# Attention and a gated recurrence on one core: own gate banks for each token half, the attention of tiles 6 and 7 ended by halves

## The reference

```python
# attention of each tile, linear form
Q, K, V = x @ Wq.T + bq, x @ Wk.T + bk, x @ Wv.T + bv
Q, K = elu(Q) + 1, elu(K) + 1
KV = einsum('bnd,bne->bde', K, V)
Z = einsum('bnd,bd->bn', Q, K.sum(axis=1) + 1e-6)
x1 = layernorm(x + (einsum('bnd,bde->bne', Q, KV) / Z[..., None]) @ Wo.T + bo)
# recurrence over the tiles; c is 512 x 128
for t in range(8):
    f = sigmoid(x1[t] @ wf.T + c @ uf.T + bf)
    i = sigmoid(x1[t] @ wi.T + c @ ui.T + bi)
    g = tanh(x1[t] @ wc.T + c @ uc.T + bc)
    c = f * c + i * g
out = layernorm(x1 + tanh(x1 @ wo.T + c @ uo.T + bo))
```

## Time and profile before

| what | us |
|---|---|
| median of 3 runs (lowest, highest) | 103.58 (103.49, 103.77) |
| the profiled execution: time | 102.75 |
| its span, first to last instruction | 101.0 |
| busy: TensorE, VectorE, ScalarE, GpSimd | 91.6, 80.9, 68.5, 42.1 |

### The profile page before, as it was taken

How to read it: one execution, slowest core, us unless ns; L and a number is a source line. 1 busy time by engine, 2 the same in 40 slices (tenths; PEclk the granted TensorE clock), 3 DMA queues, 4 the chain that set the end, 5 groups by cost and what they waited for, 6 DMA issues and landing times.

```text
span 101.0 us, 1930 instructions
## 1 busy us (share of the span) xinstructions
PE 91.6 (91%) x607; PEld 78.8 (78%) x607; DVE 80.9 (80%) x234; ACT 68.5 (68%) x143; POOL 42.1 (42%) x65
## 2 busy tenths in 40 slices
PE   5989999999799999999999999999999999896700
PEld 4859879688488978978888999989899999785300
DVE  3256598979999996898689989996455999999970
ACT  1465767587497694785869445599365949889760
POOL 2004598148358058019306704260500055455870
PEclk9999999999999999999999999999999999999998
DMA  1869999100000000000000000000000000153366
GB/s 37 295 210 295 401 394 368 46 0 3 0 0 0 0 0 0 10 0 0 0 0 0 6 0 0 0 3 3 6 0 0 0 0 0 47 168 104 104 208 208
DMA packets 5413, 7.36 MB, mean 73 GB/s; under 512 B 507, under 2 KB 3228, under 8 KB 5404
## 3 DMA queue, kind: packets, MB, share of 16 engines
q1 hardware_dynamic: 4972, 6.92, 19.4%
q10 hardware_dynamic: 432, 0.33, 1.2%
HBM read 5.15 MB, written 2.10 MB: 72 GB/s over the span
## 4 chain that ended last, share of the span: by engine, by line
PE 57%; DVE 27%; issue 5%; ACT 4%; POOL 3%; DVEq 0%; POOLq 0%; ACTq 0%
PE ps_ctx L433 7%; PE ps_k L410 6%; PE ps_q L424 6%; PE ps_ctx L453 5%; DVE stats L1140 5%; PE ps_f L397 4%; DVE x L1129 3%; DVE x L960 3%; PE ps_x L467 2%; DVE s L1011 2%; DVE x L975 2%; DVE x L1156 2%; DVE new L1004 2%; PE ps_ctx L443 2%; PE ps_f L481 2%
## 5 line engine op out<-in xcount | busy, mean ns | idle before, releaser
L346 POOL TENSOR_TENSOR s_lo<-s,s_hi 128x512 fp32r<-128x512 f32 (+1 forms) x8 | 8.1, 1012 | 24.6 <-ACT s_hi L752 24.6
L333 POOL TENSOR_TENSOR rstd<-var_eps,minus_half 128x4 f32<-128x4 f32 (+1 forms) x9 | 9.1, 1010 | 12.6 <-DVE var_eps L1148 12.6
L317 POOL TENSOR_TENSOR rstd<-var_eps,minus_half 128x4 f32<-128x4 f32 x8 | 8.6, 1078 | 6.6 <-DVE var_eps L951 6.5
L308 POOL TENSOR_TENSOR k_pair<-k_rows 128x256 f32<-128x256 f32 x8 | 6.3, 782 | 9.1 <-DVE k_rows L986 9.1
L960 DVE TENSOR_SCALAR x<-x,stats,rstd 128x128 f32<-128x128 f32 x26 | 10.0, 441 | 0.0
L805 ACT ACTIVATE x_hi<-ps_x 128x512 fp32r<-128x512 f32 x8 | 4.8, 594 | 6.2 <-PE ps_x L467 6.2
L736 ACT ACTIVATE th_f<-ps_f,half_b 128x256 f32<-128x256 f32 (+1 forms) x11 | 5.8, 530 | 4.4 <-PE ps_f L513 4.3
L410 PE MATMUL ps_k<-wkq,x_cols 128*128 128x128 f32 x64 | 8.5, 276 | 0.0
L722 ACT ACTIVATE k_exp<-ps_k,minus_one 128x512 f32<-128x512 f32 x8 | 5.5, 686 | 4.4 <-PE ps_k L418 3.5
L424 PE MATMUL ps_q<-x_cols,wkq 128*128 128x512 f32 x16 | 8.2, 593 | 0.0
L410 PEld LDWEIGHTS ps_k<-wkq,x_cols 128*128 128x128 f32 x64 | 8.0, 194 | 0.2
(11 more groups left out here) (191 smaller groups left out, 286.6 us busy)
## 6 DMA issues: line engine op xcount, KB each, us to landing
x_cols<-xt SPq DMA_DIRECT2D x8, 256.0 KB, 7.0
x_rows<-x SPq DMA_DIRECT2D x8, 256.0 KB, 7.0
out<-x SPq DMA_DIRECT2D x7, 256.0 KB, 2.2
wgate<-w_gate SPq DMA_DIRECT2D x1, 384.0 KB, 6.6
out<-x SPq DMA_DIRECT2D x2, 128.0 KB, 2.0
wkq<-w_kq ACTq DMA_DIRECT2D x1, 131.0 KB, 3.3
wvo_in<-w_vo_in ACTq DMA_DIRECT2D x1, 128.0 KB, 3.3
wout<-w_out SPq DMA_DIRECT2D x1, 128.0 KB, 6.7
```

The source lines that it names most:

```text
L308: nc.gpsimd.tensor_tensor(k_pair[:], k_rows[:, a % 2, 0:C // 2], k_rows[:, a % 2, C // 2:C], ALU.add).then_inc(k_pair_ok, 1)
L317: nc.gpsimd.tensor_tensor(rstd[:, b], var_eps[:, b], minus_half[:], ALU.pow).then_inc(rstd_ok, 1)
L333: nc.gpsimd.tensor_tensor(part_of(rstd, u, T), part_of(var_eps, u, T), minus_half[:, 0:nt * H].rearrange("p (t c) -> p t c", c=H), ALU.pow ...
L346: nc.gpsimd.tensor_tensor(s_lo[:, t % 2, part], state(t)[:, part], s_hi[:, t % 2, part].bitcast(F32), ALU.subtract).then_inc(slo_ok[k], 1)
```

## The change

- STEPS: entries 8 and 9 change places, so that (5, H, C) comes before (7, 0, H), and the halves alternate to the end.
- Gate banks: full tiles and first halves stay in ps_f, ps_i, ps_c; second halves go to the two banks of ps_ctx and to ps_k. A gate product waits for the tanh of the step before in the same banks only. The output units and out_g move to other banks, and their waits with them; both out_g use ps_i.
- Tiles 6 and 7: residual, statistics, root, normalising, turning and copies by halves, in the order HALVES. VectorE normalises the first halves, ScalarE the second.
- The low part of x1 for these tiles is made from the whole copy in SBUF: first halves on VectorE (`half_low`), second halves, and that of tile 5, on GpSimd (`x1_low`).
- The orders of all engines around them are written anew; out_x(0) and out_x(1) come later, gates_s(11) comes before out_x(2), the low part of entry 9 on VectorE goes, that of entry 8 is on GpSimd.
- GpSimd drops second_shift for units whose chunks VectorE normalises all.

```diff
 STEPS = [(0, 0, C), (1, 0, C), (2, 0, C), (3, 0, C), (4, 0, H), (5, 0, H), (4, H, C), (6, 0, H),
-         (7, 0, H), (5, H, C), (6, H, C), (7, H, C)]
+         (5, H, C), (7, 0, H), (6, H, C), (7, H, C)]
...
-SHARED_LN = (0, 6, 7)
+WHOLE = 6
+HALVES = [(6, 0), (7, 0), (6, H), (7, H)]
+
+
+SHARED_LN = (0,)
+ACT_HALVES = (2, 3)
 
 
...
-        g_bank = [ps_x1[:, 0:H * D], ps_i[:, 0:H * D]]
-        unit_bank = [ps_ctx[:, 0, :], ps_ctx[:, 1, :], ps_k[:], ps_q[:], ps_x1[:], ps_ctx[:, 0, :], ps_k[:], ps_q[:],
-                     ps_ctx[:, 1, :]]
+        g_bank = [ps_i[:, 0:H * D], ps_i[:, 0:H * D]]
+        unit_bank = [ps_f[:], ps_c[:], ps_q[:], ps_x1[:], ps_f[:], ps_c[:], ps_q[:], ps_ctx[:, 0, H * D:],
+                     ps_ctx[:, 1, H * D:]]
+        gate_bank = [[ps_f, ps_i, ps_c], [ps_ctx[:, 0], ps_ctx[:, 1], ps_k]]
...
+        def before_in_bank(k):
+
+            return max((j for j in range(k) if second_half(j) == second_half(k)), default=None)
...
+            def half_root(j):
+
+                b, c0 = HALVES[j]
+                pool.wait_ge(var_half_ok, j + 1)
+                nc.gpsimd.tensor_tensor(rstd[:, b, c0:c0 + H], var_eps[:, b, c0:c0 + H], minus_half[:, 0:H],
+                                        ALU.pow).then_inc(rstd_half_ok, 1)
+
+            def half_shift(j):
+                b, c0 = HALVES[j]
+                pool.wait_ge(minus_mean_half_ok, ACT_HALVES.index(j) + 1)
+                pool.wait_ge(rstd_half_ok, j + 1)
+                nc.gpsimd.tensor_tensor(shift[:, b, c0:c0 + H], minus_mean[:, b, c0:c0 + H], rstd[:, b, c0:c0 + H],
+                                        ALU.mult).then_inc(shift_half_ok, 1)
+
+            def x1_low(b):
+
+                if b < WHOLE:
+                    pool.wait_ge(x1c_ok, b + 1)
+                else:
+                    pool.wait_ge(x1c_half_ok, HALVES.index((b, H)) + 1)
+                nc.gpsimd.tensor_tensor(x1_lo[:, b, H * D:], x1_cols[:, b, H:C].rearrange("p c d -> p (c d)"),
+                                        x1_hi[:, b, H * D:].bitcast(F32), ALU.subtract).then_inc(x1lo_pool_ok, 1)
+
...
-            reciprocal_root(6)
-            first_shift(6)
+            half_root(0)
+            x1_low(5)
+            half_root(1)
             state_low(5)
-            reciprocal_root(7)
-            first_shift(7)
+            half_root(2)
+            half_shift(2)
+            state_low(6)
             state_low(7)
-            state_low(6)
+            half_root(3)
+            half_shift(3)
+            x1_low(6)
+            state_low(8)
+            x1_low(7)
             for u in range(len(UNITS)):
                 second_root(u)
-                second_shift(u)
+                if DVE_NORM[u] < len(blocks(u)):
+                    second_shift(u)
...
-                if k >= 1:
-                    pe.wait_ge(used, k)
-                pe.wait_ge(x1hi_ok, t + 1)
+                elif before_in_bank(k) is not None:
+                    pe.wait_ge(used, before_in_bank(k) + 1)
+                elif g == 0:
+                    pe.wait_ge(y_ok, T - 1)
+                elif g == 1:
+                    pe.wait_ge(y_small_ok, T - 1)
+                else:
+                    pe.wait_ge(y_ok, T)
+                if t < WHOLE:
+                    pe.wait_ge(x1hi_ok, t + 1)
+                else:
+                    pe.wait_ge(x1hi_half_ok, HALVES.index(STEPS[k][:2]) + 1)
...
-                pe.wait_ge(x1lo_ok, t + 1)
+                if t >= WHOLE - 1 and STEPS[k][1] == H:
+                    pe.wait_ge(x1lo_pool_ok, t - WHOLE + 2)
+                elif t >= WHOLE:
+                    pe.wait_ge(x1lo_half_ok, t - WHOLE + 1)
+                else:
+                    pe.wait_ge(x1lo_ok, t + 1)
...
+                first_done = STEPS.index((T - 1, 0, H)) + 1
                 if u == 0:
                     pe.wait_ge(out_in, 16)
-                    pe.wait_ge(y_ok, T - 1)
+                    pe.wait_ge(f_ok, first_done)
                 if u == 1:
-                    pe.wait_ge(y_small_ok, T - 1)
+                    pe.wait_ge(c_ok, first_done)
+                if u == 2:
+                    pe.wait_ge(y_small_ok, T)
+                if u == 3:
+                    pe.wait_ge(x1c_half_ok, len(HALVES))
                 if u == 4:
-                    pe.wait_ge(g_lo_ok, 1)
-                if u == 2:
-                    pe.wait_ge(y_ok, T)
-                if u == 3:
-                    pe.wait_ge(y_small_ok, T)
-                pe.wait_ge(x1c_ok, T if u >= 3 else UNITS[u][0] + UNITS[u][1])
+                    pe.wait_ge(w_ok, 1)
+                pe.wait_ge(x1c_ok, min(WHOLE, UNITS[u][0] + UNITS[u][1]))
...
             gates_x(6)
+            x1_half_turned(0)
             gates_s(6)
-            x1_turned(6)
-            out_x(0)
             gates_x(7)
+            x1_half_turned(1)
             gates_s(7)
-            x1_turned(7)
-            out_x(1)
             gates_x(8)
             gates_s(8)
             gates_x(9)
+            x1_half_turned(2)
             gates_s(9)
+            gates_x(10)
+            out_x(0)
             out_s(0)
             out_g(0)
-            gates_x(10)
             gates_s(10)
+            x1_half_turned(3)
+            out_x(1)
             add_g(1)
+            gates_x(11)
+            gates_s(11)
             out_x(2)
             add_g(2)
-            gates_x(11)
-            gates_s(11)
             out_x(3)
             add_g(3)
             out_x(4)
...
+            def half_normalise(j):
+
+                b, c0 = HALVES[j]
+                act.wait_ge(shift_half_ok, ACT_HALVES.index(j) + 1)
+                for c in range(c0, c0 + H):
+                    nc.scalar.activation(x1[:, b, c], x1[:, b, c], ACT.Identity, bias=shift[:, b, c:c + 1],
+                                         scale=rstd[:, b, c:c + 1]).then_inc(x1_half_act_ok, 1)
+
+            def x1_half_high(j):
+                act.wait_ge(x1t_half_mm, j + 1)
+                nc.scalar.activation(x1_hi[:, HALVES[j][0], half_cols(j)], ps_x1[:, half_cols(j)],
+                                     ACT.Copy).then_inc(x1hi_half_ok, 1)
+
+            def x1_half_whole(j):
+
+                b, c0 = HALVES[j]
+                nc.scalar.activation(x1_cols[:, b, c0:c0 + H].rearrange("p c d -> p (c d)"), ps_x1[:, half_cols(j)],
+                                     ACT.Copy).then_inc(x1c_half_ok, 1)
...
             gates_tanh(5)
-            first_normalise(6)
+            x1_half_high(0)
             state_high(5)
-            x1_high(6)
+            x1_half_whole(0)
             gates_tanh(6)
-            x1_whole(6)
-            first_normalise(7)
+            x1_half_high(1)
+            x1_half_whole(1)
             gates_tanh(7)
-            x1_high(7)
+            state_high(6)
             state_high(7)
-            state_high(6)
+            half_normalise(2)
             gates_tanh(8)
-            x1_whole(7)
+            x1_half_high(2)
+            x1_half_whole(2)
+            state_high(8)
             gates_tanh(9)
-            state_high(9)
+            half_normalise(3)
             out_tanh(0)
             g_high()
             gates_tanh(10)
+            x1_half_high(3)
+            x1_half_whole(3)
             out_tanh(1)
             state_high(10)
+            normalise(0)
+            gates_tanh(11)
             out_tanh(2)
-            gates_tanh(11)
-            normalise(0)
+            normalise(1)
             out_tanh(3)
-            normalise(1)
...
+            def half_low(j):
+
+                b = HALVES[j][0]
+                dve.wait_ge(x1c_half_ok, j + 1)
+                nc.vector.tensor_tensor(x1_lo[:, b, 0:H * D], x1_cols[:, b, 0:H].rearrange("p c d -> p (c d)"),
+                                        x1_hi[:, b, 0:H * D].bitcast(F32), ALU.subtract).then_inc(x1lo_half_ok, 1)
+
+            def half_statistics(j):
+
+                b, c0 = HALVES[j]
+                dve.wait_ge(y_small_ok if c0 else y_ok, b + 1)
+                nc.vector.bn_stats(stats[:, b, c0:c0 + H].rearrange("p c m -> p (c m)"),
+                                   x1[:, b, c0:c0 + H].rearrange("p c d -> p d c")).then_inc(st_half_ok, 1)
+                dve.wait_ge(st_half_ok, j + 1)
+                nc.vector.tensor_scalar(var_eps[:, b, c0:c0 + H], stats[:, b, c0:c0 + H, 2], 1.0 / D, LN_EPS, ALU.mult,
+                                        ALU.add).then_inc(var_half_ok, 1)
+                if j in ACT_HALVES:
+                    nc.vector.tensor_scalar(minus_mean[:, b, c0:c0 + H], stats[:, b, c0:c0 + H, 1], -1.0, None,
+                                            ALU.mult).then_inc(minus_mean_half_ok, 1)
+
+            def half_normalise(j):
+                b, c0 = HALVES[j]
+                dve.wait_ge(rstd_half_ok, j + 1)
+                for c in range(c0, c0 + H):
+                    nc.vector.tensor_scalar(x1[:, b, c], x1[:, b, c], mean_of(b, c), rstd[:, b, c:c + 1],
```

(67 more changed lines are left out.)

38 lines of the change are left out of this document (24 added, 14 removed).

## The result

The changed kernel took 106.38 us (median of 4, 105.94 to 107.14) against 103.53 for the kernel before (median of 4): a ratio of 1.028 (95% interval 1.022 to 1.035), 2.85 us more, where 105.9 and +2.3 were forecast. The profiled execution took 105.94 and has a span of 104.1, 3.1 more than before. TensorE's granted clock over the span was 0.981 against 0.995, but that is no cause: it was 1.00 up to 100 us, and 0.52 only from there on, when TensorE had no work left.

What follows compares the result with a forecast made beforehand. TensorE bounds the gate steps, VectorE's chain everything from the first output unit on. Entry 11's state +2.62 and the end -0.30 sum to +2.3 us; on the median of 103.58 that gives 105.9, range 105.2 to 106.5.

Steps and rivals of the forecast that it cites:

- Part 3: From entry 10's state to entry 11's: the new order puts everything in one row, 7.02 us instead of 4.75.
- Part 1: Up to the first output unit: alternating halves, own banks, halved attention give nothing; unit 0's tanh 78.20 against 78.25.
- Part 2: From unit 0's residual to entry 10's state: GpSimd's third new low part adds 0.40 us; state 0.35 later.
- Part 4: The end: second_shift dropped for units 7 and 8 lets the last root go earlier, -0.3 us.
- A: Rival on GpSimd's holds of VectorE: none for two SBUF inputs, seldom for others; +0.7, 104.3 us; chance 0.20.
- B: Rival on GpSimd's holds of VectorE: each lasts the whole instruction; +3.1, 106.7 us; chance 0.20.
- C: Rival on the steps: TensorE sets their pace, ScalarE's and VectorE's gaps absorb the rest; -0.55, 103.0 us; chance 0.12.
- D: Rival: the two effects cancel, unit 0's residual starting near 76.9; 103.4 to 103.9 us; chance 0.06.

Runs made afterwards that it cites:

- the tail put back: The changed kernel with its TensorE, ScalarE and VectorE orders after entry 10's state put back as before: 104.18 us, ratio 1.009.
- the tail put in: The kernel before with only the changed orders after entry 10's state: 105.81 us, ratio 1.021.
- the measurement of the hold: The kernel before plus 14 timings of VectorE operations beside GpSimd's subtraction, power or nothing; two SBUF inputs took 0.93 us beside a subtraction, 0.43 alone.
- both repairs: The changed kernel with old orders after entry 10's state and GpSimd's x1 low parts moved to VectorE: 103.58 us, ratio 1.001.

## Why the prediction was right, point by point

**Part 3, s(10) to s(11)**, was the main term and right to the hundredth: 7.02 us forecast, 7.02 measured, shown both ways by the tail put back and the tail put in. It isn't errors that cancel: in the trace the eight links are 0.46, 0.45, 0.48, 2.06, 0.43, 0.61, 1.67 and 0.86 us, each within 0.01 of the forecast.

**Part 1.** Forecast s(5) 64.86, s(6) 68.21, s(7) 70.54, s(8) 73.93, s(9) 76.56, tanh 78.20, residual 78.82; it was 64.64, 68.35, 69.92 (0.76 long, so as if at 70.26), 73.63 (1.01 long, as if at 74.22), 76.81, 78.55, 79.16. Three terms were mis-sized, and they partly cancel:

- VectorE's first normalise of tile 6 was given a hold of 0.31 us, to 62.95. It started at 62.71 and wasn't held. From s(5) on, with the exception below, the steps came 0.2 to 0.3 earlier than forecast.
- The tie of s(8) with GpSimd's low part at 73.62 was given to s(8). GpSimd started 0.01 us sooner and the state was held for 0.59, which turns 0.30 early into 0.29 late.
- From s(9) to the tanh it took 1.74 instead of 1.64.

The exception is s(6): it came 0.88 us after new instead of 0.53, in every trace that has the changed order there. GpSimd's power for a root ran beside it, 0.87 long instead of 0.70 (67.23 to 68.10), but what kept s(6) back stays open. It delayed nothing of size, because the next step waited for its tanh. The way of part 1 held: TensorE's freed time was lost again, in part to ScalarE's order (at most 0.46, by the run with tanh(8) ahead), in part to the holds.

One reading behind it was wrong. The prediction had the variance at 66.34 held right to GpSimd's end at 66.89, and so in full agreement with the rule of the Trainium skill (SBUF — State Buffer, the same section as under the rivals below). The same operation alone, in the kernel before:

```profile
62.38 0.17 DVE L951 TENSOR_SCALAR var_eps<-stats 128x4 f32<-128x4 f32 x1
```

At 0.57 us it went on as if begun at 66.74, which is 0.15 before GpSimd's end, like the sum at 8.36. And for that one the whole instruction would have made 0.33 us (8.36 to 8.69), not 0.26. Both rows already said what the measurement of the hold says.

**Part 2.** The hold was taken as 0.40 and is 0.54: GpSimd's low part at 81.30 came between keep and new, not between new and s. Two of the three low parts on GpSimd cost 1.1 us together (0.58 and 0.54 by the trace with them moved). The third, tile 5's at 62.25, didn't hold the normalise beside it.

**Part 4** failed: -0.3 was forecast for the dropped shift, and the end moved by 0 against s(11). VectorE's last normalise does end 0.33 earlier against s(11) (99.83 + 1.39 = 101.22; 98.45 before), GpSimd's two last roots now follow each other at 99.10. But the last store waits for something else. SyncE's issues of the last three stores, before:

```profile
97.66 0.37 SPq L290 DMA_DIRECT2D out<-x  x1
98.12 0.42 SPq L290 DMA_DIRECT2D out<-x  x1
98.63 0.40 SPq L290 DMA_DIRECT2D out<-x  x1
```

and after:

```profile
100.76 0.37 SPq L313 DMA_DIRECT2D out<-x  x1
101.22 0.42 SPq L313 DMA_DIRECT2D out<-x  x1
101.73 0.40 SPq L313 DMA_DIRECT2D out<-x  x1
```

Unit 6's store is issued when ScalarE has ended its four normalises (97.58 before, 100.68 after), and the two others behind it at 0.46 and 0.51: the last issue is 3.10 us later, as s(11) is. Before, VectorE ended at 98.45 and the issue ahead of the last one at 98.54, so the queue bound the last issue by only a tenth of a microsecond, and the chain of waits, which goes from the end back to VectorE, hid it.

**The rivals.** A, no holds for two SBUF inputs, is out by the measurement of the hold. B, the whole instruction, is out as a mechanism, though not by much: the measured holds end 0.14 to 0.26 us before GpSimd's recorded end. The Trainium skill (SBUF — State Buffer, section "SBUF: two separate sides") says that whichever of the two starts first gets the port pair for the whole instruction. Beside a subtraction the measurement agrees with it on which operations of VectorE are held and which are not; the whole instruction is too long by 0.14 to 0.26 us, some of which may be the roughness of GpSimd's spans, and for GpSimd's power of 128x4, 1.01 us long, no hold showed at all in the two pairs tried. C, TensorE sets the pace, is out: TensorE no longer lost its 1.4 us to the tanh, and unit 0's tanh came at 78.55, not at 75.7; with both repairs the kernel is the one before. D fell with the residual of unit 0 at 79.16. In the trace the growth is 3.1 us, 0.8 over the forecast: 0.34 by unit 0's start, 0.14 by the hold of part 2, 0.3 by part 4. The medians, 2.85 apart, say a little less.

By the number alone B would have won: 3.1 us is what it forecast, and the median of 106.38 is 0.3 from its 106.7 and 0.5 from the 105.9. Its terms differ from what was measured too: it put unit 0's residual at 79.40 (79.16 measured) and s(10) at 82.75 (82.44), and had the same -0.3 at the end, which didn't come. What the forecast got right is the main term, 2.3 of the 3.1 us, and the kind of the others; that the time fell within the own range, near its upper end, owes something to the holds of part 1 that cancelled.
